# First attention: a third score bank in turn, with the turned maxima in one of the three

## The reference

```
qkv = einsum('bysd,ed->byse', x, w_qkv) + b_qkv       # 16 heads
logits = einsum('bhqd,bhkd->bhqk', q, k) / sqrt(16)
attn = softmax(logits, axis=-1)
vals = einsum('bhqk,bhkd->bhqd', attn, v)
h = vals @ w_out.T + b_out
... a second attention (causal, rotary), a mixture of experts,
    a causal attention that keeps the 32 largest scores, a second mixture of experts
```

## Time and profile before

| | us |
|---|---|
| runs (3) | 1999.75, 2004.49, 2008.41; median 2004.49 |
| the profiled execution | 2008.74, of it the span 2007.0 |
| first attention: first reduction of maxima to the last `finish` | 66.47 to 310.28 |

### The profile page before, as it was taken

One profiled execution on the slowest core, in us unless ns is written; L12 is line 12 of the kernel. 1 busy time (PEld: TensorE's weight loads), 2 busy tenths in 40 slices (PEclk: granted clock), 3 DMA queues, 4 the chain that ended last, 5 costly groups with the idle time before them and its releaser, 6 DMA issues. The chain is left out here.

```text
span 2007.0 us, 35039 instructions
## 1 busy us (share of the span) xinstructions
PE 1457.3 (73%) x10387; PEld 862.3 (43%) x10420; DVE 1431.1 (71%) x4682; ACT 842.9 (42%) x2077; POOL 598.0 (30%) x1072
## 2 busy tenths in 40 slices
PE   7788887978787640999953487677667666666664
PEld 4222224534444430566632254454445444444553
DVE  5778885667777640111138799999999999899971
ACT  3366664225555410222212344455445554454442
POOL 3300000230000005000025334545555554555541
PEclk9799998979999965999986556767787777776776
DMA  5472120331221602111135210300030002200000
GB/s 165 115 242 56 53 66 9 85 104 48 61 49 32 250 15 87 40 42 47 42 118 144 62 28 14 85 16 9 27 76 29 9 27 55 72 2 12 1 1 13
DMA packets 81760, 120.87 MB, mean 60 GB/s; under 512 B 9112, under 2 KB 67392, under 8 KB 80836
## 3 DMA queue, kind: packets, MB, share of 16 engines
q1 hardware_dynamic: 78340, 110.60, 19.1%
q0 software_dynamic: 3264, 8.41, 1.3%
HBM read 74.11 MB, written 45.38 MB: 60 GB/s over the span
## 5 line engine op out<-in xcount | busy, mean ns | idle before, releaser
L1657 DVE MATCH_REPLACE8 top_left<-top_next,top_left 128x65 f32<-128x65 f32 (+15 forms) x768 | 321.8, 426 | 0.0
L1652 DVE MAX8 top_next<-top_left 128x8 f32<-128x65 f32 (+15 forms) x768 | 300.4, 431 | 0.1
L1565 POOL TENSOR_TENSOR top_e<-top_e,top_left 128x129 f32<-128x129 f32 (+15 forms) x256 | 191.3, 769 | 200.4 <-DVE top_left L1657 200.3
L1382 ACT ACTIVATE top_e<-top_ps_s,top_neg_max 128x129 f32<-128x129 f32 (+15 forms) x256 | 125.8, 492 | 189.7 <-POOL top_neg_max L1550 176.2
L735 DVE TENSOR_REDUCE tok_rowmax<-tok_ps_s 128x1 f32<-128x512 f32 x256 | 167.1, 688 | 32.8 <-PE tok_ps_s L577 30.2
L2213 DVE TENSOR_TENSOR moe_hid<-moe_act_gate,moe_ps_h 128x512 f32<-128x512 f32 x39 | 26.8, 687 | 219.9 <-ACT moe_act_gate L2174 219.9
L1226 PE MATMUL top_ps_pt<-ident,top_e 128*128 128x128 f32 x640 | 141.9, 351 | 24.9 <-issue 14.6
L735 DVE TENSOR_REDUCE rot_rowmax<-rot_ps_s 128x1 f32<-128x128 f32 (+3 forms) x256 | 115.6, 487 | 44.6 <-PE rot_ps_s L580 41.0
L708 ACT ACTIVATE tok_et<-tok_ps_st 128x1024 f32<-128x1024 f32 x128 | 124.3, 1021 | 53.2 <-PE tok_ps_st L611 53.2
L2113 PE MATMUL moe_ps_h<-moe_w,moe_rows_t 128*128 x312 | 141.8, 597 | 0.2 <-issue 0.2
L1394 ACT ACTIVATE top_prob_t<-top_ps_pt 128x128 f32<-128x128 f32 (+3 forms) x256 | 104.9, 431 | 70.7 <-PE top_ps_pt L1226 69.8
(11 more groups left out here) (342 smaller groups left out, 3135.2 us busy)
## 6 DMA issues: line engine op xcount, KB each, us to landing
moe_w<-in_moe_w SPq DMA_DIRECT2D x3, 4096.0 KB, 24.0
moe_xs<-zeros SPq DMA_DIRECT2D x1, 5120.0 KB, 20.7
last_xs<-zeros SPq DMA_DIRECT2D x1, 5120.0 KB, 33.7
moe_rows<-moe_xs SPq DMA_DIRECT2D x40, 128.0 KB, 2.2
moe_ys<-moe_y SPq DMA_DIRECT2D x38, 128.0 KB, 1.7
top_vs<-v_by_position SPq DMA_DIRECT2D x16, 256.0 KB
k_parts<-rot_parts SPq DMA_DIRECT2D x16, 192.4 KB, 3.2
rot_ks<-k_parts SPq DMA_DIRECT2D x16, 192.4 KB
```

Source lines behind the costliest of these rows:

```text
L1382: act.activation(e[:, U % KEPT, 0:keys(U)], row(U), ACT.Exp, bias=neg_max[:, U % 4:U % 4 + 1]).then_inc(e_ok, 1)
L1565: pool.tensor_tensor(e[:, U % KEPT, 0:w], e[:, U % KEPT, 0:w], left[:, U % 4, 0:w], ALU.subtract).then_inc(prob_ok, 1)
L1652: dve.max(next8[:, U % 2, step // 2, :], left[:, U % 4, 0:keys(U)]).then_inc(pick, 1)
L1657: ins = dve.match_replace(left[:, U % 4, 0:w], next8[:, U % 2, step // 2 - 1, :], left[:, U % 4, 0:w], 0.0)
```

## The change

`ps_s` gets three banks when `causal` is false; `ps_cls`, used there only for `neg_t`, goes, and `neg_t` becomes half of bank 0 of `ps_s`. Function `bank(u)` says which bank a unit takes: units 0, 1, 2 take 1, 2, 1; from unit 3 on they take 0, 1, 2 in turn. Unit 15 is in bank 0, then the turned maxima, then unit 3 of the next group. `bank_free` has the waits: most units now wait for the reduction three before them; units 2 and 4 for the one two before, unit 5 for the one four before; unit 3 waits for the four copies of the turned maxima (`nt_out`). The table of PE's order changes with it. The second attention keeps its form.

```diff
-FIRST_PASS = {False: ((1, 1, 1), (1, 1, 1, 0), (1, 1, 1, 0), (1, 1, 1, 1)),
+FIRST_PASS = {False: ((0, 1, 1), (1, 1, 1, 1), (1, 1, 1, 1), (1, 1, 1, 0)),
...
-        ps_s = c.psum(st, f"{tag}_ps_s", [P, 2, S])
+        ps_s = c.psum(st, f"{tag}_ps_s", [P, 2 if causal else 3, S])
...
+            neg_t = ps_s[:, 0, :].bitcast(BF16)[:, 0:S]
...
+        def bank(u):
+            if causal:
+                return u % 2
+            return (1, 2, 1)[u] if u < EARLY else (u - EARLY) % 3
+
+        def bank_free(pe, b, g, u):
+            if causal:
+                pe.wait_ge(max_ok, b * (G * units) + (g * units + u + 1))
+            elif u == EARLY:
+                if not (isinstance(b, int) and b == 0 and g == 0):
+                    pe.wait_ge(nt_out, b * (G * HG) + g * HG)
+            else:
+                ahead = {0: 3, 1: 3, 2: 2, 4: 2, 5: 4}.get(u, 3)
+                pe.wait_ge(max_ok, b * (G * units) + (g * units + u - ahead + 3))
...
-                    pe.wait_ge(max_ok, b * (G * units) + (g * units + u + 1))
+                    bank_free(pe, b, g, u)
```

More of the change, by code:

```diff
@@ L486, in attend @@
         ps_st = c.psum(st, f"{tag}_ps_st", [P, HG, S])
-        ps_s = c.psum(st, f"{tag}_ps_s", [P, 2, S])
+        ps_s = c.psum(st, f"{tag}_ps_s", [P, 2 if causal else 3, S])
         ps_pv = c.psum(st, f"{tag}_ps_pv", [P, S])
-        ps_cls = c.psum(st, f"{tag}_ps_cls", [P, S])
-        neg_t = ps_cls[:, :].bitcast(BF16)[:, S:]
+        if causal:
+            ps_cls = c.psum(st, f"{tag}_ps_cls", [P, S])
+            neg_t = ps_cls[:, :].bitcast(BF16)[:, S:]
+        else:
+            neg_t = ps_s[:, 0, :].bitcast(BF16)[:, 0:S]
         ctx_t = ps_pv[:, :].rearrange("p (n h s) -> p n h s", h=HG, s=STRIP)
@@ L574, in score_units @@
                         pe.wait_ge(loaded[g % G], b * (16 * NLOADS) + 16 * NLOADS * (g // G + 1))
-                    pe.wait_ge(max_ok, b * (G * units) + (g * units + u + 1))
+                    bank_free(pe, b, g, u)
                     lhs = q[0:PARTS * HD, h, qt * P:qt * P + P]
-                    mm = pe.matmul(ps_s[:, u % 2, 0:keys(qt)], lhs, k[0:PARTS * HD, h, k0:k0 + keys(qt)],
+                    mm = pe.matmul(ps_s[:, bank(u), 0:keys(qt)], lhs, k[0:PARTS * HD, h, k0:k0 + keys(qt)],
                                    start=True, stop=not causal)
                     if causal:
-                        mm = pe.matmul(ps_s[:, u % 2, qt * P:qt * P + P], c.ident_bf[:, :], c.mask_qk[:, :],
+                        mm = pe.matmul(ps_s[:, bank(u), qt * P:qt * P + P], c.ident_bf[:, :], c.mask_qk[:, :],
                                        start=False, stop=True)
@@ L734, in maxima @@
                     dve.wait_ge(s_mm, b * (G * units) + (g * units + u + 1))
-                    dve.tensor_reduce(rowmax[:, g % 2, u:u + 1], ps_s[:, u % 2, 0:keys(qt)], AX_X, ALU.max
+                    dve.tensor_reduce(rowmax[:, g % 2, u:u + 1], ps_s[:, bank(u), 0:keys(qt)], AX_X, ALU.max
                                       ).then_inc(max_ok, 1)
```

## The result

The changed kernel takes 2019.58 us (median of 9 runs, 2015.63 to 2024.95), the kernel before 2011.3 us in the same comparison (9 runs, 1999.75 to 2015.37). The ratio is 1.0057, interval 1.0043 to 1.0071: about 11.5 us slower. In microseconds the interval is +8.6 to +14.3. The time lies in the range of the forecast (1999 to 2021), but the forecast held no measurable change the likeliest, its +7.4 us lie under this interval, and the kernel is measurably slower. The profiled execution took 2017.75 us, its span 2016.0.

A forecast was written before the change was run, and what follows sets the result against it. No engine is full; a chain through DVE, PE and the exps sets each 14.18 us step. Terms +12.2, +0.4, -0.9 and -4.3 sum to +7.4 us: 2016.1 us profiled, 2012 us on the median; range 1999 to 2021 us.

The forecast's parts named there:

- prologue: First 16 reductions, before the loop: with a third bank their units are ready ahead, -0.9 us.
- step 0: First loop step: it has no division, so only the two further units count, +0.4 us.
- steps 1 to 14, undisturbed: Loop steps with both the late division and the two further units: 14 x 0.87 = +12.2 us.
- the stall of step 3 goes: PE's 1.63 us wait for keys behind the fills of zeros, and the low clock after it, vanish: -4.3 us.
- clock spells: Stretches at granted clock 0.50 in the loop: no term in the forecast's sum, left to rival D.
- Unit 3 behind the first pair: In PE's row before the division: division and values of block 0 come later, 0.43 us a step.
- the two further units in PE's row: Between the values of block 0 and the pair of block 3, where PE has no gap: 0.44 us a step.
- rival D: Added PE idle before values lowers the clock in each of 14 steps: +48 us, 2053 us; chance 0.04.
- the same row of work: Tail from the last values to the next step's first exp: claimed to keep its 3.40 us.

The follow-up runs named there:

- e3: Changed kernel plus five extra 512-column matmuls a step, results unused, where PE idles before the copies of the maxima; ratio 1.0012 to the kernel before.
- e4: Kernel before with the two fills of zeros issued after the stage's last loads; ratio 0.9967 to the kernel before.
- e5: e3 with units 8 and 12 back in their old places in PE's order; ratio 0.9990 to the kernel before.
- e6: e5 with DVE's division after unit 5 and not after unit 6; ratio 0.9985 to the kernel before.
- e2: Changed kernel with the old table of PE's order, so only the three banks and the maxima in bank 0 remain; ratio 1.0012 to the kernel before.
- e12: e9 without the five extra matmuls in the tail; ratio 0.9968 to the kernel before.
- e9: e6 with the fills of zeros issued after the stage's last loads; ratio 0.9944 to the kernel before.
- e1: Kernel before with only the new table of PE's order, two score banks kept; ratio 1.0102 to the kernel before.
- e11: Kernel before (two banks, old order) with the fills of zeros late and the division after unit 5; ratio 0.9975 to the kernel before.
- e8: e1 with the five extra matmuls a step in the tail; ratio 1.0049 to the kernel before.

## Why the prediction was right and wrong

In the profiled executions the stage grew by 257.27 - 243.81 = 13.46 us. Step by step of the forecast:

| term | forecast | measured | from |
|---|---|---|---|
| prologue | -0.9 | -1.0 | first reduction to first exp, 14.89 and 13.90 |
| step 0 | +0.4 | +1.0 | 15.03 and 15.99 |
| steps 1 to 14, undisturbed | +12.2 | +10.8 | e3 209.32 less e4 198.50 |
| the stall of step 3 goes | -4.3 | -4.0 | before 202.52 less e4 198.50 |
| clock spells | 0 | +6.7 | after 216.00 less e3 209.32 |
| sum | +7.4 | +13.5 | |

*Right: the steps, the prologue and the stall.* Unit 3 behind the first pair makes the division late by 0.44 us (2.35 to 2.79 us; the values of block 0 at 3.66, forecast 3.65), and the two further units in PE's row make the exps of block 3 late by 0.87 (8.57, forecast 8.6); e5 shows the second, e6 that the division's place is on the path. The step came out at 14.96, not 15.05, since the last values follow the last exp after 0.05 us where they took 0.14 before. The prologue gained what was said, and the stall went: PE comes to these keys 13.90 us after their issue (137.86 and 123.96), where before it was ready for them after 9.61 and got them after 11.24. The wait follows the pace: none at steps of 14.96 us, 0.96 us at 14.62 (e5), 1.63 at 14.18, 4.55 at 13.96 (e6).

*Wrong: the clock term, set to zero.* The step that failed is the price of rival D, of which the forecast said: "It decides once the added idle reaches the 1.63 us that came on top of the tail there; I count 0.3 near the tail and 0.43 far from it". Three things were wrong in it. The condition was too high: the runs show spells behind idle pieces of 1.12 us (e2) and about 1.2 us (the changed kernel), some 0.6 us more than before and far from 1.63 more. The count missed that unit 3, moved out of the tail, leaves one such piece where there were shorter ones (the forecast called the tail "the same row of work", which is true of DVE and not of PE). And the rival was all or nothing, 14 spells or none, at 0.04, while the clock falls in some steps: four in the changed kernel's profile, three besides the stall's in e2's, two in e12's. e3 takes the 6.7 us away by filling that idle time, and e2 shows that the new order is not needed: with unit 3 behind the copies there are spells, at the step's old length of 14.18 us. With this term the sum would have been +14 us, and slower the likeliest. Why the clock falls in some of these steps and not in others stays open.

The Trainium skill, TensorE: Matmul & The Clock Gate, section A second HAM failure mode: psum-queue depth-cycling, tells of a kernel whose clock swung because TensorE idled briefly between its groups of matmuls while it cycled through PSUM banks. The forecast named it and gave it little because of the earlier trace rows. The traces of e2 and of the changed kernel, with their windows at 0.50, agree with the page in that small idle pieces are enough; the piece here is the wait for the copies of the maxima and not for a bank. Clock 1.00 in one execution before was no evidence for a kernel whose idle pieces are longer.

*A smaller miss:* step 0 became 1.0 us longer and not 0.4. It runs partly at clock 0.50 anyway, and its length is 14.66, 15.77 and 15.45 us in e6, e9 and e12, whose undisturbed steps agree; I can't say what of it is the change's.

*Outside the stage* the profiled span is 4.5 us shorter after (1.7 ahead of it, 2.7 behind). The part behind the stage ranges from 1690.9 to 1700.8 us over the profiles of all kernels here, and its code is the same, so I take this for scatter. Between the stage's +13.5 and the +11.5 us of the timed ratio nothing needs explaining.

*Luck.* The profiled execution came to 2017.75 us, 1.7 over the 2016.1 of the forecast, and that closeness is luck: the stage grew by 6.1 us more than the sum said, and the rest of the span happened to be 4.5 us shorter. The median, 2019.58, lies 7.6 us over the forecast of 2012 and just inside the range; the forecast started from the 2004.49 us of three runs, where nine give 2011.3.

## What to carry to other kernels

A gap that repeats on an engine is worth a buffer only if the chain that ends the step runs through it: here three banks gave steps of 13.96 us when the order let DVE divide earlier (e6; 14.18 before), and 14.96 when the order put two more units into PE's row. Before moving work out of a stretch in which TensorE waits, measure what idle piece it leaves, since the clock may fall behind it in some steps and not in others; one profile with clock 1.00 does not show that a kernel is safe from it (e1). A wait on a DMA with a landing of its own does not scale with the pace: price it by when the data land.

## What the runs showed of the hardware

- The granted clock fell to 0.50 where TensorE went on behind an idle piece of about 1.1 to 1.2 us, in some steps of the stage: four spells in the changed kernel's profile, three in e2's, two in e12's. With the piece at about 0.6 us (the kernel before apart from its stall, e4, e11) or filled (e3, e5, e8, e9) it did not fall there in any profile. A spell cost about 1.4 to 1.7 us, by its steps against the same steps of e3, e4 and e9.
- It is not regular: the changed kernel and e1 have the same order and an idle piece of 1.2 us, and their profiled executions had four spells and none.
- Useless matmuls in a wait made the kernel faster: 1.0057 to 1.0012 (e3), 1.0102 to 1.0049 (e8).
- A reduction that reads a 128x512 bank starts 0.62 us after the one before where its data are ready, and 0.69 where they come just in time: the prologue's 16 took 11.05 us with two banks and 10.05 with three.
